# A two-layer decoder on one core: first self attention's early steps put in another order, the output bias added later, and part of cross attention's first trip moved from VectorE to ScalarE

## The reference

```python
x = _layernorm(x + _L0_attn_ref(x, Wq, bq, Wk, bk, Wv, bv, Wo, bo))   # causal, 32 heads of 16, output bias bo
x = _layernorm(x + _L0_xattn_ref(x, ctx_4096, ctx_4096))               # autocorrelation by Fourier transform
x = _layernorm(x + _L0_ffn_ref(x, base_W, gate_W, lora_A, lora_B))     # mixture of 28 low-rank experts
x = _layernorm(x + _L1_attn_ref(x, Wqkv, ..., Wout))                   # causal, 32 heads, ALiBi
x = _layernorm(x + _L1_xattn_ref(x, ctx_4096, Wq, Wk, Wv, Wo))         # cross attention: 16 heads of 96, 4 key groups
x = _layernorm(x + _L1_ffn_ref(x, A, B, Wr, br))

# inside _L1_xattn_ref, hidden being context and latents joined (256 tokens)
scores = jnp.einsum('bkgqd,bksd->bkgqs', q, k) * scale
attn = jax.nn.softmax(scores, axis=-1)
out = jnp.einsum('bkgqs,bksd->bkgqd', attn, v)
```

## Time and profile before

| | us |
|---|---|
| median of three runs (range) | 859.44 (859.24 to 859.6) |
| the profiled execution's own time | 861.57 |
| span of its trace | 859.8 |
| PE busy | 825.5 (96%) |
| DVE busy | 578.5 (67%) |
| ACT busy | 431.0 (50%) |
| POOL busy | 260.7 (30%) |
| PE's first matmul starts at | 7.33 |

### The profile page before, as it was taken

The page is one execution under the profiler, slowest core; times in us unless marked ns, Lnnn a source line. Parts: engine busy times, 40 slices in busy tenths (PEclk is TensorE's granted clock), DMA queues, the critical chain, the costliest instruction groups (busy, mean ns, idle before and its releaser), DMA issues.

```text
span 859.8 us, 22670 instructions
## 1 busy us (share of the span) xinstructions
PE 825.5 (96%) x9312; PEld 683.3 (79%) x9312; DVE 578.5 (67%) x1515; ACT 431.0 (50%) x1105; POOL 260.7 (30%) x310
## 2 busy tenths in 40 slices
PE   6999999999999999999998998999999999999996
PEld 6888887675547787777777787989998899889983
DVE  5665755677886676677776546884677567756776
ACT  4453444558763343465555445444653475347532
POOL 1221313559976532112222567710000100010001
PEclk9999999999999999999999998999999999999998
DMA  9311001313220200000000122320000010000001
GB/s 310 132 38 29 16 21 28 105 53 87 72 61 26 74 21 8 21 24 23 18 19 18 31 61 88 101 61 26 1 2 2 2 50 2 2 2 25 2 2 50
DMA packets 20998, 36.77 MB, mean 43 GB/s; under 512 B 3200, under 2 KB 7424, under 8 KB 20640
## 3 DMA queue, kind: packets, MB, share of 16 engines
q1 hardware_dynamic: 20800, 35.20, 13.4%
q10 hardware_dynamic: 96, 0.13, 0.1%
HBM read 30.86 MB, written 2.10 MB: 38 GB/s over the span
## 4 chain that ended last, share of the span: by engine, by line
PE 80%; DVE 10%; ACT 4%; issue 2%; POOL 2%; DMA 1%; SPq 1%; ACTq 0%; POOLq 0%; DVEq 0%
PE bank L827 17%; PE bank L829 16%; PE bank L828 16%; PE bank L987 6%; PE bank L1261 6%; PE bank L1008 3%; PE bank L1125 2%; DVE tank L2554 2%; PE bank L957 2%; PE bank L992 2%; PE bank L1112 1%; DVE tank L2564 1%; DVE tank L2334 1%; PE bank L1280 1%; PE bank L846 1%
## 5 line engine op out<-in xcount | busy, mean ns | idle before, releaser
L827 PE MATMUL bank<-wr,hTl 128*128 128x512 f32 (+4 forms) x400 | 154.8, 387 | 1.3 <-issue 0.8
L829 PE MATMUL bank<-wr,hTh 128*128 128x512 f32 (+4 forms) x400 | 148.2, 371 | 0.0
L828 PE MATMUL bank<-wr,hTh 128*128 128x512 f32 (+4 forms) x400 | 147.9, 370 | 0.0
L1564 ACT ACTIVATE pT<-bank 128x512 f32<-128x512 f32 x128 | 70.0, 605 | 97.5 <-PE bank L957 97.5
L2334 DVE TENSOR_REDUCE tank<-bank 128x4 f32<-128x512 f32 x128 | 82.1, 684 | 42.6 <-PE bank L957 42.6
L827 PEld LDWEIGHTS bank<-wr,hTl 128*128 128x128 f32 (+1 forms) x400 | 75.1, 188 | 18.5 <-issue 5.5
L829 PEld LDWEIGHTS bank<-wr,hTh 128*128 128x128 f32 (+1 forms) x400 | 75.2, 188 | 12.2
L828 PEld LDWEIGHTS bank<-wr,hTh 128*128 128x128 f32 (+1 forms) x400 | 75.3, 188 | 11.0 <-issue 1.0
L827 PE MATMUL bank<-hTh,wr 128*128 128x256 f32 (+1 forms) x272 | 82.0, 302 | 0.2 <-DVE hTl L2525 0.2
L828 PE MATMUL bank<-hTl,wr 128*128 128x256 f32 (+1 forms) x272 | 81.2, 298 | 0.0
L829 PE MATMUL bank<-hTh,wr 128*128 128x256 f32 (+1 forms) x272 | 81.1, 298 | 0.0
(11 more groups left out here) (254 smaller groups left out, 2007.2 us busy)
## 6 DMA issues: line engine op xcount, KB each, us to landing
raw<-w_qkv_dram SPq DMA_DIRECT2D x12, 256.0 KB, 2.8
raw<-w_xq_dram SPq DMA_DIRECT2D x16, 192.0 KB, 2.4
raw<-w_xo_dram SPq DMA_DIRECT2D x12, 256.0 KB, 2.8
cin<-xT_dram SPq DMA_DIRECT2D x8, 256.0 KB, 3.3
x_all<-x_dram SPq DMA_DIRECT2D x8, 256.0 KB, 7.3
cin<-ctx_dram SPq DMA_DIRECT2D x8, 256.0 KB, 3.0
cin<-ctxT_dram SPq DMA_DIRECT2D x8, 256.0 KB, 2.9
out_dram<-x_all SPq DMA_DIRECT2D x8, 256.0 KB, 2.0
```

Of the source, the lines that this page charges most:

```text
L827: mm(dst, lhs[1], rhs[0], start=start, stop=False)
L828: mm(dst, lhs[0], rhs[1], start=False, stop=False)
L829: return mm(dst, lhs[0], rhs[0], start=False, stop=stop)
L1564: av(pT[e][:, 2 * rows + n, :], t_bank[n][:, :], ACT.Exp).then_inc(exp_ready, 1)
```

## The change

Three things in layer 0's attention. `half_of_values` goes: the values of batches 0 and 1 are whole projections after steps 5 and 6, in 12 matmuls of 128x512 each. The two tiles of `part_of_pair(0, 2)`, which stood together after step 9, stand one after step 8 and one after step 9. The splits of batches 4 and 5 move from steps 7 and 8 to steps 6 and 7, and with them on SP the loads that follow. The first output bias waits until DVE has written all four groups of rows of batch 0.

Two things in cross attention's first trip. In g = 0, slot 1, DVE makes the four reciprocals in one instruction and multiplies the first two blocks only; ACT multiplies the other two (`first_norm`), placed behind its splits of the queries. In g = 1, slot 0, ACT and not DVE copies the turned tiles out of PSUM.

```diff
+        def copied_by_act(trip, s, g):
+            return (s, g) == (1, 0) or (trip, s, g) == (0, 0, 1)
...
             elif kind == "v":
-                now, n, limit = r == 2 if at_end else not even and r in (1, 3), b - (r == 1), B
+                now, n, limit = r == 2 if at_end else not even and r in (1, 2 if b == 1 else 3), b - (r == 1), B
             elif kind == "x":
-                now, n, limit = b > 0 and r == (0 if even else 3), b + 3, B
+                now, n, limit = b > 2 and r == (0 if even else 3) or b == 1 and r > 1, b + 3 + (b == 1 and r == 3), B
...
             attention_step(0, 5)
-            half_of_values(0, 0)
-            half_of_values(0, 1)
             attention_step(0, 6)
-            half_of_values(1, 0)
             attention_step(0, 7)
-            half_of_values(1, 1)
-            for i in range(8, DRAIN):
+            attention_step(0, 8)
+            part_of_pair(0, 2, (0,))
+            attention_step(0, 9)
+            part_of_pair(0, 2, (1,))
+            for i in range(10, DRAIN):
...
                 for i in range(2):
                     pe.wait_ge(xpn_ready[s], nth(trip, 2 * XKV, 2 * g + i + 1))
+                    if (trip, s, g, i) == (0, 1, 0, 1):
+                        pe.wait_ge(first_normed, 1)
...
+            def first_norm():
+                act.wait_ge(first_sums, 1)
+                for j in range(2, 4):
+                    block = xp[1][:, j * XT:(j + 1) * XT]
+                    ins = av(block, block, ACT.Copy, scale=st[1][:, ROWSUM.start + j:ROWSUM.start + j + 1])
+                ins.then_inc(first_normed, 1)
...
             def add_bias(b):
+                if b == 0:
+                    pool.wait_ge(qk_rows, batch(0, 0, 2, 2))
...
+            def norm_beside_act():
+                dve.wait_ge(xp_ready[1], 2)
+                both_sums = st[1][:, ROWSUM.start:ROWSUM.start + 4]
+                v.reciprocal(both_sums, both_sums).then_inc(first_sums, 1)
+                dve.wait_ge(first_sums, 1)
+                for j in range(2):
+                    block = xp[1][:, j * XT:(j + 1) * XT]
+                    ins = v.tensor_scalar(block, block, st[1][:, ROWSUM.start + j:ROWSUM.start + j + 1], None, ALU.mult)
+                ins.then_inc(xpn_ready[1], 2)
```

More of the change, by code:

```diff
@@ L416, in decoder @@
         xpn_ready = per_slot("xpn_ready")
+        first_sums = sem("first_sums")
+        first_normed = sem("first_normed")
         xpT_psum = per_slot("xpT_psum")
@@ L887, in projected @@
                 bank_taken(u)
+                if l == 0:
+                    pe.wait_ge(w0_ready, W0_TILES + 2)
                 for k in range(KT):
@@ L919, in part_of_pair @@
                 if 1 in tiles_of_part:
[L920 to L931, removed]
                     ins.then_inc(m_full[u % 2], 1)
@@ L1043, in attention_step @@
                     rows_turned(l, 0, b + 1)
-                if of_step(l, i, "v") is not None and (l, i) not in ((0, 5), (0, 7)):
+                if of_step(l, i, "v") is not None:
                     projected(l, "v", of_step(l, i, "v"))
@@ L1051, in attention_step @@
                 for n, kind in enumerate(PARTS):
-                    if of_step(l, i, kind) is not None and of_step(l, i, kind) > 1:
+                    if of_step(l, i, kind) is not None and of_step(l, i, kind) > 1 and (n, of_step(l, i, kind)) != (0, 2):
                         part_of_pair(n, of_step(l, i, kind))
@@ L1775, in cross_probs, with probsT_by_act @@
                     ins.then_inc(xp_ready[s], 1)
-            def first_probsT(trip):
+            def first_norm():
[4 more added lines that the diff above has]
+                ins.then_inc(first_normed, 1)
+            def probsT_by_act(trip, s, g):
                 for i in range(2):
-                    act.wait_ge(xpT_psum[1], nth(trip, 2 * XKV, i + 1))
-                    copy(xpT[1][:, i * 512:(i + 1) * 512], bank[1][i][:, :]).then_inc(xpT_ready[1], 1)
+                    act.wait_ge(xpT_psum[s], nth(trip, 2 * XKV, 2 * g + i + 1))
+                    copy(xpT[s][:, i * 512:(i + 1) * 512], bank[s][i][:, :]).then_inc(xpT_ready[s], 1)
             def cross_heads(trip, s, g):
@@ L1907, in _ @@
                         each(route_exp, trip - 1)
-                    if g == 0:
-                        first_probsT(trip)
+                    if (trip, g) == (0, 0):
+                        first_norm()
+                    for s in both:
+                        if copied_by_act(trip, s, g):
+                            probsT_by_act(trip, s, g)
                     for s in both:
@@ L2554, in cross_probsT @@
                     v.tensor_copy(xpT[s][:, i * 512:(i + 1) * 512], bank[s][i][:, :]).then_inc(xpT_ready[s], 1)
+            def norm_beside_act():
[7 more added lines that the diff above has]
+                ins.then_inc(xpn_ready[1], 2)
             def cross_norm(trip, s, g):
+                if (trip, s, g) == (0, 1, 0):
+                    return norm_beside_act()
                 for i in range(2):
@@ L2731, in _ @@
                     if g > 0:
-                        each(cross_probsT, trip, g)
+                        for s in both:
+                            if not copied_by_act(trip, s, g):
+                                cross_probsT(trip, s, g)
                     if g + 1 == XKV and behind:
```

## The result

| | before | after |
|---|---|---|
| median, us (range, runs) | 859.29 (857.5 to 860.34, 13) | 856.72 (854.56 to 858.41, 13) |
| the profiled execution's own time | 861.57 | 854.56 |
| span of its trace | 859.8 | 852.8 |

The ratio is 0.9968, with a 95% interval of 0.9959 to 0.9977: 2.6 us faster, where 6.5 were forecast. The time, 856.72, lies 0.5 us outside the range given. The two profiled executions differ by 7.0 us, close to the forecast sum. But that of before was slower than every one of its 13 timed runs, and that of after was the fastest of its own. So the forecast came near for a pair of executions that is not the usual pair, which is luck, and the question is what the usual ones hold.

What follows compares the result with a forecast made beforehand. PE, busy 825.5 of 859.8 us, was taken as the bound. Terms 0.7 + 1.0 + 1.7 + 2.8 + 0.3 = 6.5 us off 859.44 gave 853.0 us; own range 852.0 to 854.0, 8-in-10 range 851.9 to 856.2.

Steps and rivals of the forecast that it cites:

- Output bias later: First scores, layer 0: DVE's row instruction no longer stretched by POOL's bias, so PE's wait goes; 0.7 us saved.
- Steps 5 to 9: Layer 0's attention: moved matmuls cover the 1.28 us wait before step 9's scores, 0.27 us returns; 1.0 us saved.
- Cross attention, g = 0: First trip: DVE loses a reciprocal and a multiplication pair to ACT, so its copies begin earlier; 1.7 us saved.
- The clock: Around 530 us, first trip: shorter PE waits keep the clock at 2.4 GHz, so `cross_values` runs faster; 2.8 us saved.
- The first rival: Clock drop absent from timed runs or still coming, so only 3.7 us saved, 855.7 us; chance 0.17.
- Cross attention, g = 1: First trip: ACT takes DVE's two copies of slot 0, so PE's wait before the product goes; 0.3 us saved.
- Behind both places: After the early steps and the cross attention edits: PE's own work sets the pace, so the saving reaches the end; no loss.

Runs made afterwards that it cites:

- before_again: The kernel before, unchanged, run once more for a second trace; 859.07 us.
- after_again: The changed kernel, unchanged, run once more for a second trace; 856.97 us, ratio 0.9977 to before.
- cross_again: Repeat of the kernel before with only the edits of cross attention's first trip, for a second trace; 856.81 us.
- early_only: The changed kernel without its cross attention edits, so only those in layer 0's attention; 857.98 us, ratio 0.9984 to before.
- before_fed: The kernel before plus 20 unread identity transposes filling PE's three waits in cross attention's first g = 0; 859.34 us, ratio 0.9996.
- no_copy_g1: The changed kernel with DVE, not ACT, copying slot 0's turned tiles in g = 1; 857.13 us, ratio 0.9973 to before.
- cross_only: The kernel before with only the edits of cross attention's first trip; 858.26 us, ratio 0.9986 to before.

## Why the prediction was wrong, step by step

The usual execution is read here from before_again against after_again, with the other traces of the same code as a check.

*Output bias later, 0.7 forecast.* The mechanism held: no wait at the first scores, and no stretch at the new place, in any of the traces with this edit. But the 0.7 us too belonged to the first profiled execution. In the four other traces with the old order PE waits 0 to 0.15 us there. In before_again the third row instruction takes 1.00 us and not 1.74, and the first scores start without idle time:

```profile
22.75 1.16 PE L987 MATMUL bank<-qk 32*128 32x128 f32 x16
```

A gain can't be read: s0 lies at 21.8 to 23.9 us in the five traces without the edit and at 22.1 to 24.2 in the nine with it. cross_again has no stretched pair although its bias is the old one (on POOL it came at 23.04 us, behind the rows), so the old order didn't always collide. What the half brings beyond the next step, 1.4 - 0.9 = 0.5 us, lies between -0.3 and 1.2 by the interval of early_only, and no run shows that it is this.

*Steps 5 to 9, 1.0 forecast.* Right. s0→T0 is 503.3 to 503.8 us in five traces without it (mean 503.5), 502.1 to 502.9 in those with it (mean 502.6): 0.9 us. The residual wait of 0.28 us before L946 is the 0.27 that was subtracted.

*Cross attention, g = 0, 1.7 forecast.* T0→V0 was 4.97 to 5.10 us and is 3.62 to 3.75: 1.3 to 1.4 in eight of ten traces, and 2.2 in two. DVE's remaining pair (L2575) decides: 0.62 us in the trace of after, 1.69 in after_again, beside a POOL subtraction. The step took the split L2541 as the thing at risk, and missed that the pair kept on DVE can be stretched like the one taken away. It also had ACT's two multiplications out of the way in 0.8 us; they take 0.91, and in the trace of after they are what the second half of the transposes waits for, 0.58 us.

*The clock, 2.8 forecast: the first step that failed.* It took the slow stretch of one profiled execution as what all executions contain. The clock is now at 1.00 there, as forecast, but the usual execution had less to lose: V0→T1, which holds the slow matmuls, is 16.69 us in before, 14.95 in before_again and 15.60 in early_only, against 13.93 in after and after_again. So 2.8 us is what the stretch lost in the first trace and 1.0 what it lost in before_again. And before_fed shows that removing the drop alone gives nothing that the runs can tell (1.2 us at most), since PE then waits for DVE. Groups g = 1 as a whole, with the clock and the copy by ACT, gained 17.5 - 15.8 = 1.7 us, where 3.1 had been forecast for both. The text's own remark, that the three timed runs agree within 0.36 us and so contain the same, was right, but what they contained need not be this drop (they have no trace; by before_again it was the shorter one); the 2.13 us between profile and median, read as leaving this open, was the sign: of the 2.5 us between the spans of the two traces of before, 1.4 are this stretch and 1.1 the start. The first rival, "the clock gives nothing" (855.7 us), was nearer.

The Trainium skill (TensorE: Matmul & The Clock Gate, "The HAM clock gate") was quoted for a window that runs free of the kernel, by which the same waits could slow one run and not another. The traces agree in that the same program shows drops of different length, 5.35 us at 0.50 in one execution and 0.55 and 0.89 in two stretches of 3 us in another. They don't show an execution without a drop: before, before_again and early_only, the three with the old g = 0 and nothing fed, all have one. Even so the rival that hangs on that rule should have had more than its 0.17.

*Cross attention, g = 1, 0.3 forecast.* 0.2 at the place (no_copy_g1), 0 at the end.

*Behind both places, nothing forecast: the second step that failed.* The text said "behind both places PE's own work sets the pace, so I expect the saving to arrive at the end"., from which it was read, end at 560 us, and the product of g = 2 begins at 567.7 us in before, so they could not show that place. Nothing waits there in before either, but the reason was that PE came there late. With PE early, the copies of g = 2 are late by 1.3 to 1.8 us in four of the five traces in which DVE still makes them beside POOL (all but cross_only). g = 2 costs 16.2 to 16.4 us in the traces of before, and 17.2 to 18.2 in those of after.

The sum for the usual execution (before_again against after_again) is: s0→T0 0.9, T0→V3 50.86 - 49.61 = 1.25, end 0; that is 2.15, and with up to 0.5 for what the early half brings beyond it 2.2 to 2.7, against 2.6 measured. The two executions themselves differ by less, 1.2 us (859.07 and 857.85), since s0 of after_again came 0.8 us later. By group, T0→V3 is 1.3 at g = 0, 1.8 at g = 1 and -1.8 at g = 2. Against the forecast, 1.7, 3.1 and 0, the clock with the copy falls 1.3 us short and what was put at nothing 1.8; with 0.4 at g = 0 and 0.3 in the early part this is the 3.9 us between 6.5 and 2.6.

For the two profiled executions the same columns give 0.9 + 1.3 + 4.4 + 0.4 = 7.0 us. There g = 1 gained 3.2, as forecast, and g = 2 lost 1.0, which was not. A larger gain at g = 0 (2.2), at the start and at the end made up for the loss, so the sum is near 6.5 partly because errors cancelled.

The range called the bounds of the terms, 852.0 to 854.0 us, is not theirs either: with the bias at 0.7 and the clock at 2.8 the other terms' bounds give 5.2 to 6.8 us, that is 852.6 to 854.2.

## What to carry to other kernels

A term that rests on a clock drop needs a second profile or the spread of the runs behind it: when the profiled execution is slower than every timed run, its rarest feature is the first thing to distrust. When a wait is shortened, follow the engine that was waited for to the next places where it is needed, and ask which other stream (here DMA-paced weight splits) doesn't move along: that nothing waited there may have been owed to the delay. And after such a change, look whether an idle engine can take the queued copy, which here moved the ratio from 0.9968 to 0.9945.

## What the runs showed of the hardware

DVE's multiplication of 128x256 by a column of factors, SBUF to SBUF with one tensor input, takes 0.35 us alone and up to 1.46 beside POOL's splits; the minimum and median of sixteen hardly show it (346/354/1453 ns), only the maximum does, and with POOL held back all sixteen lie between 347 and 354 ns. The Trainium skill (SBUF — State Buffer, "SBUF: two separate sides") describes the shared ports as "an exclusive lock, not a bandwidth split", which a maximum of 0.35 us plus nearly the whole of POOL's 1.29 us agrees with: the longest lose 1.1 us. DVE's maxima from PSUM (0.68 us) kept their length beside the same POOL instructions.

A PE kept busy with transposes that nothing reads kept its clock (1.00 in place of 0.50 or 0.55) and yet gained no time that 12 runs could tell (ratio 0.9986 to 1.0005). The clock's cost at one place is then not additive with the waits around it.

How often the clock drops can be read in part from the mean granted clock of each timed run. The end of the kernel lowers it too, but to no less than 0.996 in the eleven traces that have no other drop. A mean of 0.995 or less stands in 22 of the 63 runs of before for which it is on record, and in 5 of the 12 of early_only; in before_fed it stands in none of 12, and in one of 77 of the kernels with the edits of cross attention. The 22 took 860.1 us in the mean and the other 41 859.1. The 0.992 of the first profiled execution came back in two of the 63 (860.67 and 861.65 us), so the long drop seems to be rare. Left open is how often the short one comes, since before_again, which has it, reads 0.996.
